# Linear attention and routed FFN: h^T k before Wv, diagonal blocks masked four at a time, residual sums on GpSimd

## The reference

```python
h = layernorm(x)
q = elu(h @ Wq + bq) + 1;  k = elu(h @ Wk + bk) + 1;  v = h @ Wv + bv      # per head
k = k / sqrt(sum(k * k, depth) + 1e-6)
attn = (q @ k^T) @ v                    # no softmax: q @ (k^T v)
y = h + attn @ Wo + bo
x1 = x + layernorm(y) * gamma + beta
h3 = layernorm(x1)
score = h3 @ w_router                   # keep the 768 highest of 1024 in each batch
out = x1 + where(kept, gelu(h3 @ w_block), h3)
```

## Time and profile before

| what | value |
|---|---|
| time, median of 3 runs | 97.76 us (96.92 to 98.74) |
| profiled execution, its own time | 97.48 us |
| its span, first to last instruction | 95.5 us |
| TensorE busy | 85.9 us |
| VectorE busy | 85.3 us |
| ScalarE busy | 67.3 us |
| GpSimd busy | 61.5 us |
| mean granted TensorE clock | 0.979 of full |

### The profile page before, as it was taken

The page is one execution under the profiler, slowest core; times in us unless marked ns, Lnnn a source line. Parts: engine busy times, 40 slices in busy tenths (PEclk is TensorE's granted clock), DMA queues, the critical chain, the costliest instruction groups (busy, mean ns, idle before and its releaser), DMA issues.

```text
span 95.5 us, 2547 instructions
## 1 busy us (share of the span) xinstructions
PE 85.9 (90%) x870; PEld 74.5 (78%) x870; DVE 85.3 (89%) x252; ACT 67.3 (71%) x174; POOL 61.5 (64%) x114
## 2 busy tenths in 40 slices
PE   4997899899999999999999999999879999999500
PEld 1344559797979996997799999999779997969400
DVE  4328999999999999999999999999999999999750
ACT  5004299897997775668593788759988969698900
POOL 5154189999990185760975799998999898402400
PEclk9999999999999999999999999999999999999965
DMA  1999799999989970000000000000000006104386
GB/s 34 262 297 302 181 288 293 283 173 130 147 97 134 140 93 0 0 0 0 0 7 0 0 0 3 0 0 7 0 0 7 0 3 190 37 0 117 110 253 186
DMA packets 18114, 9.01 MB, mean 94 GB/s; under 512 B 819, under 2 KB 18102, under 8 KB 18102
## 3 DMA queue, kind: packets, MB, share of 16 engines
q1 hardware_dynamic: 12704, 6.23, 24.2%
q0 software_dynamic: 4160, 2.10, 19.9%
q10 hardware_dynamic: 1238, 0.53, 1.9%
HBM read 4.66 MB, written 2.10 MB: 71 GB/s over the span
## 4 chain that ended last, share of the span: by engine, by line
PE 48%; DVE 21%; POOL 12%; issue 5%; DMA 5%; ACT 2%; ACTq 2%; DVEq 1%
PE bank L1129 10%; PE bank L1204 6%; PE bank L1145 6%; PE bank L1120 5%; DMA x_sb<-in_L_attn_x_dram 5%; PE bank L1165 5%; PE bank L1164 5%; DVE norm_sb L722 4%; DVE bn L713 4%; POOL r L361 3%; DVE x_sb L874 3%; POOL x_sb L376 3%; DVE beats L856 2%; PE bank L1183 2%; PE bank L1224 2%
## 5 line engine op out<-in xcount | busy, mean ns | idle before, releaser
L1129 PE MATMUL bank<-w_c,hT 128*128 128x128 f32 x120 | 15.3, 276 | 0.0
L1129 PEld LDWEIGHTS bank<-w_c,hT 128*128 128x128 f32 x120 | 14.3, 192 | 0.9 <-ACT hT L466 0.7
L376 POOL TENSOR_TENSOR x_sb<-x_sb,xb_sb 128x512 f32<-128x512 f32 x8 | 10.5, 1324 | 5.7 <-ACT x_sb L537 5.4
L544 ACT ACTIVATE norm_sb<-xb_sb,shift,gain 128x128 f32<-128x128 f32 x32 | 13.1, 487 | 0.0
L1165 PE MATMUL bank<-back,hT 128*128 128x128 f32 x64 | 12.4, 275 | 0.0
L1164 PE MATMUL bank<-M_sb,qT 128*128 128x128 f32 x64 | 12.4, 275 | 0.0
L843 DVE TENSOR_SCALAR beats<-s_row,s_col 128x896 bf16<-128x896 f32 (+6 forms) x28 | 12.0, 477 | 0.0
L537 ACT ACTIVATE x_sb<-bank,r 128x128 f32<-128x128 f32 x32 | 9.4, 375 | 3.0 <-DVE s_col L823 2.9
L856 DVE SCALAR_TENSOR_TENSOR beats<-s_row,s_col,later 128x128 bf16<-128x128 f32 x32 | 10.0, 371 | 0.0
L1165 PEld LDWEIGHTS bank<-back,hT 128*128 128x128 f32 x64 | 9.7, 192 | 0.0
L1164 PEld LDWEIGHTS bank<-M_sb,qT 128*128 128x128 f32 x64 | 9.7, 192 | 0.0
(11 more groups left out here) (117 smaller groups left out, 212.7 us busy)
## 6 DMA issues: line engine op xcount, KB each, us to landing
xb_sb<-in_L_attn_x_dram SPq DMA_DIRECT2D x4, 512.0 KB, 6.8
xb_sb<-beta_sb POOLq DMA_DIRECT2D x4, 512.0 KB, 7.2
out_dram<-x_sb SPq DMA_DIRECT2D x7, 256.0 KB, 2.3
x_sb<-in_L_attn_x_dram SPq DMA_DIRECT2D x6, 256.0 KB, 5.7
x_sb<-in_L_attn_x_dram SPq DMA_DIRECT2D x2, 128.0 KB, 2.9
x_sb<-in_L_attn_x_dram ACTq DMA_DIRECT2D x1, 256.0 KB, 4.7
out_dram<-x_sb SPq DMA_DIRECT2D x1, 128.0 KB, 3.1
out_dram<-x_sb ACTq DMA_DIRECT2D x1, 128.0 KB, 3.1
```

Source lines behind the costliest of these rows:

```text
L376: nc.gpsimd.tensor_tensor(x_sb[:, a:a + TH], x_sb[:, a:a + TH], xb_sb[:, a:a + TH], ALU.add).then_inc(gelu_sums, 1)
L544: last = nc.scalar.activation(norm_sb[:, t], xb_sb[:, t], ACT.Identity, bias=shift3[:, t:t + 1], scale=gain3[:, t:t + 1])
L1129: last = nc.tensor.matmul(o[:, t * P:(t + 1) * P], hT[:, u, t * P:(t + 1) * P], w_c[:, vector * P:(vector + 1) * P], start=True, stop=True)
```

## The change

- Values: `v_proj` and `scale_v` are gone. The keys, not the values, are multiplied by their norms, in place in SBUF (`scale_k`, 8 on VectorE by `KEYS_BY`). `attention_matrix(b)` now adds h^T k, from `norm_sb` and `k_sb`. ScalarE copies that (`copy_hk`), a new `values(b)` on TensorE multiplies it by Wv, and `mask_vk`, `attention_out` and `copy_M` follow as before. `k_sb` has a place for every unit, and no ring.
- Biases: column 127 of h is replaced by ones (each row of h sums to zero, so its last value follows from the others), and the weights are folded to match. `LIFT`, `spread_bo` and the addition in `copy_hT` go. `fold_biases` comes ahead of the first transposes on TensorE, `copy_w` ahead of `first_copy(0)` on ScalarE, and `bn_x(1)` ahead of `first_normalise(0)` on VectorE.
- Comparisons: `compare(b, J, 1)` starts at its own diagonal block, with 1024, 896, ... 128 columns for eight tiles. `mask_own(b, half)` multiplies four diagonal blocks by the triangle in one bfloat16 instruction, in place.
- Residuals: `X1_BY` is 'S' for all units, so `y_gamma` goes, the `residual` of VectorE becomes `scale_y`, and GpSimd gets seven more residual additions.
- The lists of all engines and `BANK_USES` are written anew. The masks of GpSimd come ahead of the four `add_beta`.

In VectorE's new list, what follows `x1_stats(5)` is, with c for compare, mo for mask_own and sc for score_cols: c(0,0) c(0,1) sc(2) c(0,2) c(0,3) y_stats(6) c(0,4) sc(2) c(0,5) c(0,6) c(0,7) mo(0,0) sc(3) scale_y(6) sc(3) scale_y(7) mo(0,1) sc(4) sc(4) x1_stats(6) c(1,0) to c(1,5) drop_last(0) mo(1,0) sc(5) drop_first(0) merge(0) c(1,6) c(1,7) x1_stats(7) mo(1,1) sc(5) c(2,0) c(2,1) merge(1) c(2,2) c(2,3) drop_first(1) c(2,4) c(2,5) sc(6) sc(6) merge(2) mo(2,0) drop_last(1) sc(7) sc(7) c(2,6) c(2,7) merge(3) mo(2,1) c(3,0) to c(3,3) mo(3,0) drop_first(2) c(3,4) to c(3,7) merge(4) mo(3,1) and then the last drops and merges.

```diff
     NORM1 = 'DDDADDDA'
     ROOT_GROUPS = ((0,), (1,), (2, 3), (4, 5), (6, 7))
-    WIDE = (0, 1, 2, 3)
+    OWN_BY = 'DDDD'
+    KEYS_BY = 'DDDDDDDD'
     Y_STATS = 'ADADDDDA'
-    X1_BY = 'SGGGGGGG'
+    X1_BY = 'SSSSSSSS'
     NORM3 = 'AAAAAAAA'
...
+        hk_sb = sb("hk_sb", [P, B, P])
...
+        def scaled_keys(u):
+
+            a = TH * HEADS * (u % 2)
+            keys = k_sb[:, u].rearrange("p t (h e) -> p (t h) e", e=DEPTH)
+            return keys, keys, k_rnorm[:, u // 2, a:a + TH * HEADS].unsqueeze(2).to_broadcast([P, TH * HEADS, DEPTH])
...
+        def own_blocks(b, half):
+
+            rows = beats[:, b % 2, TH * half:TH * half + TH].rearrange("p j c -> p (j c)")
+            a = TH * half * P
+            blocks = rows[:, a:a + (TH - 1) * (T + 1) * P + P]
+            return bass.AP(tensor=blocks.tensor, offset=blocks.offset, ap=[blocks.ap[0], [(T + 1) * P, TH], [1, P]])
...
+                nc.gpsimd.memset(to_last[:, 0:P - 1], 0.0)
+                nc.gpsimd.memset(to_last[:, P - 1:P], 1.0)
+                nc.gpsimd.memset(less_last[:, P - 1:P], 0.0)
...
             roots1(2)
             shifts1(2)
             roots1(3)
+            roots1(4)
+            shifts1(4)
+            masks()
             add_beta(0)
-            roots1(4)
             add_beta(1)
-            masks()
             add_beta(2)
-            shifts1(4)
             add_beta(3)
             roots2(0)
             roots2(1)
             residual(0)
+            residual(1)
             roots3(0)
+            roots3(1)
             affine3(0)
             roots2(2)
+            affine3(1)
             roots2(3)
-            roots3(1)
-            affine3(1)
+            residual(2)
+            residual(3)
             roots3(2)
+            roots3(3)
+            affine3(2)
+            affine3(3)
             roots2(4)
             roots2(5)
+            residual(4)
+            residual(5)
             gelu_sum(0)
-            roots3(3)
+            roots3(4)
             gelu_sum(1)
-            gelu_sum(2)
-            roots3(4)
-            affine3(2)
-            affine3(3)
-            affine3(4)
-            roots3(5)
-            gelu_sum(3)
             roots2(6)
             roots2(7)
+            residual(6)
+            residual(7)
+            roots3(5)
+            gelu_sum(2)
+            affine3(4)
+            gelu_sum(3)
             gelu_sum(4)
+            roots3(6)
+            roots3(7)
             gelu_sum(5)
             affine3(5)
-            roots3(6)
-            roots3(7)
             affine3(6)
             affine3(7)
...
             def copy_hT(u):
                 act.wait_ge(h_full, u)
-                nc.scalar.activation(hT[:, u], bank_of(("h", u)), ACT.Identity, bias=lift[:, 0:1]).then_inc(hT_done, 1)
+                nc.scalar.copy(hT[:, u], bank_of(("h", u))).then_inc(hT_done, 1)
...
+            def copy_hk(b):
+                act.wait_ge(hk_full, b + 1)
+                nc.scalar.copy(hk_sb[:, b], bank_of(("M", b))[:, 0:P]).then_inc(hk_done, 1)
+
             def copy_M(b):
                 act.wait_ge(M_full, b + 1)
-                nc.scalar.copy(M_sb[:, b], bank_of(("M", b))[:, P:2 * P]).then_inc(M_done, 1)
+                nc.scalar.copy(M_sb[:, b], bank_of(("M", b))[:, 2 * P:3 * P]).then_inc(M_done, 1)
...
-                nc.vector.memset(lift[:], LIFT)
+                nc.vector.memset(norm_sb[:, :, P - 1:P], 1.0)
-            def spread_bo():
-
-                dve.wait_ge(bo_in, 16)
-                dve.wait_ge(ident_set, 1)
-                nc.vector.tensor_scalar(bo_diag[:], ident[:], LIFT * D, bo_col[:, 0:1], ALU.mult, ALU.add).then_inc(bo_set, 1)
...
-            def scale_v(u):
-                a = TH * HEADS * (u % 2)
-                dve.wait_ge(v_full, u + 1)
+            def scale_k(u):
                 dve.wait_ge(rnorm_done, u // 2 + 1)
-                if u >= KRING:
-                    dve.wait_ge(vk_full, (u - KRING) // 2 + 1)
-                nc.vector.tensor_tensor(v_sb[:, u % KRING].rearrange("p t (h e) -> p (t h) e", e=DEPTH),
-                                        bank_of(("v", u)).rearrange("p (n e) -> p n e", e=DEPTH),
-                                        k_rnorm[:, u // 2 % 2, a:a + TH * HEADS].unsqueeze(2)
-                                        .to_broadcast([P, TH * HEADS, DEPTH]), ALU.mult).then_inc(v_done, 1)
+                out_keys, keys, norms = scaled_keys(u)
+                nc.vector.tensor_tensor(out_keys, keys, norms, ALU.mult).then_inc(keys_dve, 1)
 
             def mask_vk(b):
                 if b == 0:
                     dve.wait_ge(mask_set, 1)
                 dve.wait_ge(vk_full, b + 1)
...
             def compare(b, J, part):
 
-
-                c0 = P * (J + 1) if part == 0 or b in WIDE else max(P * (J + 1), HW)
-                c1 = HW if part == 0 else T * P
                 s_J = s_col[:, T * b + J:T * b + J + 1]
-                dve.wait_ge(s_row_done, 2 * b + part + 1)
-                if b >= 2 and J == 0 and (part == 0 or b in WIDE):
+                dve.wait_ge(s_row_done, 2 * b + 2)
+                if b >= 2 and J == 0:
                     dve.wait_ge(first_full, b - 1)
                     dve.wait_ge(last_full, b - 1)
-                ins = nc.vector.tensor_scalar(beats[:, b % 2, J, c0:c1], s_row[:, b, c0:c1], s_J, None, ALU.is_le)
-                if part == 1 and J in (TH - 1, T - 2):
+                ins = nc.vector.tensor_scalar(beats[:, b % 2, J, P * J:T * P], s_row[:, b, P * J:T * P], s_J, None, ALU.is_le)
+                if J in (TH - 1, T - 1):
                     ins.then_inc(beats_done, 1)
 
-            def compare_own(b, half):
+            def mask_own(b, half):
 
                 if b == 0 and half == 0:
                     dve.wait_ge(mask_set, 1)
-                dve.wait_ge(s_row_done, 2 * b + half + 1)
-                if b >= 2 and half == 0:
-                    dve.wait_ge(first_full, b - 1)
-                    dve.wait_ge(last_full, b - 1)
-                for I in range(TH * half, TH * half + TH):
-                    last = nc.vector.scalar_tensor_tensor(out=beats[:, b % 2, I, I * P:(I + 1) * P],
-                                                          in0=s_row[:, b, I * P:(I + 1) * P],
-                                                          scalar=s_col[:, T * b + I:T * b + I + 1], in1=later[:],
-                                                          op0=ALU.is_le, op1=ALU.mult)
-                last.then_inc(own_done, 1)
+                dve.wait_ge(beats_done, 2 * b + half + 1)
+                o = own_blocks(b, half)
+                nc.vector.tensor_tensor(o, o, later16[:].unsqueeze(1).to_broadcast([P, TH, P]), ALU.mult).then_inc(own_dve, 1)
...
             def attention_matrix(b):
-                pe.wait_ge(k_done, 2 * b + 2)
-                pe.wait_ge(v_done, 2 * b + 2)
+                pe.wait_ge(*keys_set(2 * b))
+                pe.wait_ge(*keys_set(2 * b + 1))
                 o = take(("M", b))
                 for t in range(T):
-                    u = 2 * b + t // TH
-                    last = nc.tensor.matmul(o[:, 0:P], v_sb[:, u % KRING, t % TH], k_sb[:, u % KRING, t % TH],
+                    last = nc.tensor.matmul(o[:, 0:P], norm_sb[:, T * b + t], k_sb[:, 2 * b + t // TH, t % TH],
                                             start=(t == 0), stop=(t == T - 1))
-                last.then_inc(vk_full, 1)
+                last.then_inc(hk_full, 1)
+
+            def values(b):
+                pe.wait_ge(hk_done, b + 1)
+                nc.tensor.matmul(bank_of(("M", b))[:, P:2 * P], w_c[:, 2 * P:3 * P], hk_sb[:, b], start=True,
+                                 stop=True).then_inc(vk_full, 1)
...
             busy_start()
+            fold_biases()
             first_transpose(0)
-            fold_biases()
             first_transpose(1)
             first_keys(0)
             first_keys(1)
@@ -1255,106 +1288,102 @@
             q_proj(0)
             k_proj(1)
             q_proj(1)
-            fold_back()
-            v_proj(0)
-            centre_wz()
-            v_proj(1)
             transpose_h(2)
             transpose_h(3)
-            transpose_h(4)
+            centre_wz()
             k_proj(2)
             k_proj(3)
+            transpose_h(4)
+            q_proj(2)
+            transpose_h(5)
+            q_proj(3)
+            transpose_h(6)
             k_proj(4)
-            v_proj(2)
-            transpose_h(5)
-            q_proj(2)
-            transpose_h(6)
             k_proj(5)
+            attention_matrix(0)
+            fold_back()
+            values(0)
             k_proj(6)
-            attention_matrix(0)
-            q_proj(3)
             attention_out(0)
-            v_proj(3)
+            transpose_h(7)
             y_half(0)
             y_half(1)
```

More of the change, by code:

```diff
@@ L616, in _ @@
             exp_q_half(7)
-            copy_xT(1)
             gelu(0, 0)
+            norm_sum(1)
             gelu(0, 1)
```

(98 more changed lines are left out.)

378 lines of the change are left out of this document (195 added, 183 removed), and 16 rows, old and new, of the table BANK_USES.

## The result

| | kernel before | changed kernel |
|---|---|---|
| time, median | 97.53 us (96.92 to 98.74, 4 runs) | 99.86 us (99.38 to 101.14, 4 runs) |
| ratio to before | | 1.024 (95% interval 1.013 to 1.036) |
| the same, on a second chip | 97.67 us | 99.56 us, ratio 1.021 (1.016 to 1.025) |

Some executions of one kernel take over 1.5% longer than its fastest; the ratios leave these out, the medians keep them.

The account below looks back on a forecast made before the run. TensorE bounds up to 50 us, then mostly VectorE and GpSimd. x1_stats(5) at 57.7 us, plus 28.1 of last stage and 5.7 of standing still, puts the last merge at 91.5; plus 5.5 gives 97.0 us, range 91.8 to 100.2.

Parts of the forecast that it names:

- rival B: Last stage: GpSimd's roots3 comes 3 to 4 us later than forecast and scores wait for it; 100.7 us, chance 0.17.
- TensorE and the first half: Up to x1_stats(5): TensorE 6.3 us less work, y_half(0) at 28.2 us, GpSimd without idle time, x1_stats(5) ending at 57.7.
- VectorE's prices: VectorE's instructions: mask_own 0.4 us, scale_k 678 ns, comparisons 0.52 ns a column; in sum 9.3 us less work.
- The standing still: Last stage: comparisons, masks and merges stop beside GpSimd's additions, adding 5.7 us, between 5.3 at best and 7.8.
- Rival A: Last stage: GpSimd's additions do not hold up the comparisons, or only slightly; 92.3 us, chance 0.30.
- That leaves 28.1 us: Last stage, x1_stats(5) to last merge: 32.9 us before, less removed VectorE instructions, plus new ones, gives 28.1 us.
- three score_cols: Last stage: three score_cols come into it on VectorE, adding 0.4 us.
- start of the stage: Last stage begins when x1_stats(5) ends, at 57.7 us.
- from last merge to the end of the execution: After the last merge: 5.5 us more to the end, 3.55 of output DMA and 1.98 around the span.

Follow-up runs that it names:

- e_head: Changed kernel with the old order at the head put back on VectorE, TensorE and ScalarE: 1.020 of the kernel before, profiled execution 99.07 us.
- e_resid: Changed kernel with the residual sums of units 1 to 7 put back on VectorE: 1.027 of the kernel before.
- e_portfree: Changed kernel with GpSimd's eight gelu_sums replaced by six-column powers about as long, output incomplete: 0.975 of the kernel before.
- b_own: Kernel before with only the comparisons changed: diagonals within compare, mask_own in place of compare_own: 1.011 of the kernel before.
- e_fill: Changed kernel, gelu_sums 2 to 7 on VectorE, score_cols(5,1) followed by merge(1) and unit 2's sum ahead of compare(2,0): 96.29 us, 0.988 of before.
- e_early: Changed kernel with the second half of score_cols(5) and its round trip through TensorE put earlier: 1.008 of the kernel before.

## Why the prediction was wrong

The forecast was 0.5 to 0.8% faster, and the kernel is 2% slower. The 99.86 us lie inside the range of 91.8 to 100.2 us, which had been drawn wide for rival B, so that is no merit of the mechanism.

**TensorE and the first half: right.** y_half(0) at 28.34 us in e_head (28.2 predicted), GpSimd in the chain of waits without a break from 36.7 to 72.8 us in the profiled execution of the result, x1_stats(5) released by GpSimd's residual and ending at 58.11 us in e_head (57.7). e_resid shows that both engines stand about level there.

**VectorE's prices: right.** mask_own 0.409 us (0.4), scale_k 0.702 (0.678), comparisons by the slope: 0.676 us for 896 columns as before.

**The standing still: right, and about its size.** From e_portfree to e_head the comparisons' means grow by 4.0 us in sum (20.6 against 16.6 us) and seven merges by 1.1 us. That is 5.1 us, against 5.7 predicted. Net it is 4.0 us of the stage, since e_portfree has 1.1 us more of waits (4.0 against 2.9), which the standing still had covered. Rival A, the second likeliest, is refuted.

**The step that failed** is "That leaves 28.1 us". It took the stage of before, 32.9 us, and subtracted what VectorE no longer does, as if every instruction removed took its time with it and no new wait came. In the undisturbed stage of e_portfree 32.4 us are left, 4.3 us more. Of these 3.2 us are waits: 4.0 us, where the stage of before has the 0.8 us that the sum had kept. In e_head's stage, 28.1 + 5.1 of standing still leaves 3.2 of the 36.4 us. VectorE's waits there are 2.9 us (2.0 for scores, 0.7 for row sums, 0.2 for TensorE's z), 2.1 us more than before.

The other 1.1 us lie mostly in the subtraction itself. Instructions of VectorE overlap by nearly 0.1 us: compare_own(0, 1) has 1.13 us in the timeline before, but the next comparison starts 1.05 us behind it, at 61.86. From each start to the next, the instructions removed from the stage took 10.3 us (compare_own 8.3, the rest 2.0), and the prediction took away 11.1. It let three score_cols come in where there are two, 0.1 us the other way. Some 0.4 us stay unassigned.

The waits are new because of the order. In the kernel before:

```profile
60.81 1.13 DVE L856 SCALAR_TENSOR_TENSOR beats<-s_row,s_col,later 128x128 bf16<-128x128 f32 x4
...
69.53 0.22 DVE L823 TENSOR_TENSOR s_col<-bank,r 128x2 f32<-128x2 f32 x2
...
74.00 1.66 DVE L843 TENSOR_SCALAR beats<-s_row,s_col 128x256 bf16<-128x256 f32 x4
```

score_cols(5) stands at 69.53 us, and the first comparison of batch 2 is the third of the four at 74.00, so over 4 us of other work lie between. In batch 3 score_cols(7) at 80.90 us and the first comparison at 83.16 have compare_own(3, 0) between them, which needs only the first half of the row. In the new list compare(2,0) follows score_cols(5,1) directly, and the row goes by way of TensorE and ScalarE while VectorE waits 1.36 us; nothing in it can start on half a row. That list stood written out in the section on the change, and the prediction named a wait at score_cols only for rival B, there as GpSimd's fault. b_own shows the same without any other part of the change: 2.1 us less busy time, 2.0 us more waits behind x1_stats(5) and 0.8 just ahead of it, and 1.1% slower. e_fill shows that the longest wait is a gap and not the bound of another engine. For the end of the stage this isn't shown: in e_portfree the chain of waits runs almost wholly over TensorE and ScalarE from 80.2 us on.

**The sum with the measured terms.** 97.0 + 0.4 (start of the stage) + 3.2 (the waits and the rest) - 0.6 (less standing still) - 1.0 (from last merge to the end of the execution 4.5 us in e_head, not 5.5) gives 99.0 us; e_head's profiled execution was 99.07. The 3.2 us that the subtraction missed, most of them waits, turn a forecast of slightly faster into 2% slower. Rival B had this time (100.7), but by another way: GpSimd's late roots3 never stopped a score in e_head or in the changed kernel, where score_cols (L872) waits 0.2 us in the whole stage, and for TensorE.

## What to carry over

Don't price a stage by subtracting instructions from its length. Write the new order down, and for every instruction that needs a round trip over other engines count the work that stands between request and use; what is short of the trip's length is a wait, and independent work such as a merge can be put there at no cost (1.3 us of it in e_fill). Take what an instruction occupies from its start to the next start, not from its busy time. When work moves to an engine that makes another stand still, ask what it will lie beside: the same eight additions cost 0.4 us in one order and 4.3 us in the other.

## What the runs showed of the hardware

A predicated copy on VectorE stands still beside a 128x512 addition of GpSimd as a comparison does (1.71 against 0.74 us); I had rows for compare_own alone. A power of six columns, which keeps GpSimd busy for as long, holds up nothing: with eight of them no merge was longer than 0.743 us. In the other direction a power of four columns, 1.01 us when alone, takes 1.49 us beside comparisons in the changed kernel, and 2.12 us once in e_early:

```profile
70.19 1.49 POOL L412 TENSOR_TENSOR r<-var,minus_half 128x4 f32<-128x4 f32 x1
```

The Trainium skill ("SBUF — State Buffer", Who interferes with whom) ties the standing still to VectorE instructions with two SBUF inputs or in a two-port mode. The comparisons stand still here as by that rule: six of them take 4.15 us beside an addition and 3.23 without. Its list of operations doesn't name the predicated copy, which reads two tensors in SBUF, `dropped` and `norm_sb`; the 1.71 us fit the first case.
